# When a part's first expert block is let in, in a fused graph layer and mixture-of-experts kernel on one Trainium2 core

## The reference, cut to what matters

```
h   = layernorm(x)
agg = segment_sum(h[src] * edge_weight, dst)          # 12500 x 256
x   = x + agg @ W.T + b
z   = layernorm(x)
p   = softmax(z @ gate_w + gate_b); keep the two largest of 8 per node
for e in experts:  acc += cw[:, e] * (gelu(z @ W1[e] + b1[e]) @ W2[e] + b2[e])
x   = x + acc
```

## Time and profile before

| | us |
|---|---|
| median of the three runs | 2642.3 |
| the profiled execution, its time | 2648.2 |
| its span | 2646.6 |
| its mean granted clock of PE | 0.897 |
| PE busy / DVE busy / POOL busy | 2072.6 / 1590.4 / 1809.6 |
| ACT busy / PEld busy | 655.6 / 1629.8 |

### The profile page before, as it was taken

The page is one execution under the profiler, slowest core; times in us unless marked ns, Lnnn a source line. Parts: engine busy times, 40 slices in busy tenths (PEclk is TensorE's granted clock), DMA queues, the critical chain, the costliest instruction groups (busy, mean ns, idle before and its releaser), DMA issues.

```text
span 2646.6 us, 46928 instructions
## 1 busy us (share of the span) xinstructions
PE 2072.6 (78%) x11178; PEld 1629.8 (62%) x11179; DVE 1590.4 (60%) x6566; ACT 655.6 (25%) x1900; POOL 1809.6 (68%) x1909
## 2 busy tenths in 40 slices
PE   4665686698789788887985999886879878887585
PEld 2444464486577676665863778764667666665474
DVE  7888445365365365364563554675776756685475
ACT  2332121132122132221221223221222222223121
POOL 7665777777767767767766666767777777751473
PEclk8767898899899899998998999998989889998797
DMA  8766756877858768768768679677789797886697
GB/s 286 244 199 208 238 165 189 264 224 229 265 182 290 240 197 275 251 206 280 231 221 253 210 249 319 216 248 238 258 292 305 230 304 254 282 248 198 224 305 248
DMA packets 304350, 646.04 MB, mean 244 GB/s; under 512 B 62536, under 2 KB 197226, under 8 KB 291402
## 3 DMA queue, kind: packets, MB, share of 16 engines
q1 hardware_dynamic: 145320, 325.55, 36.4%
q0 software_dynamic: 90384, 248.17, 31.5%
q10 hardware_dynamic: 68370, 69.23, 7.5%
HBM read 543.70 MB, written 208.20 MB: 284 GB/s over the span
## 4 chain that ended last, share of the span: by engine, by line
PE 27%; DVE 20%; DMA 16%; SPq 15%; issue 11%; POOL 9%; ACT 1%; DVEq 1%; ACTq 0%; POOLq 0%
SPq L500 13%; DMA slots<-stage 10%; PE bank L881 9%; POOL rows L519 8%; PE bank L974 7%; PE bank L958 6%; DMA stage<-sorted_x 3%; DVE spread L1362 2%; DVE bn L1341 1%; PE bank L901 1%; POOL got L560 1%; DMA xi<-slots 1%; SPq L450 1%; PE bank L945 1%; DVE square_n L1409 1%
## 5 line engine op out<-in xcount | busy, mean ns | idle before, releaser
L519 POOL DMA_INDIRECT rows<-xhat,src_t x1488 | 1428.1, 960 | 561.3 <-issue 441.1
L881 PE MATMUL bank<-rows,spread 128*80 128x256 f32 x3328 | 869.7, 421 | 150.0 <-issue 77.9
L881 PEld LDWEIGHTS bank<-rows,spread 128*80 128x80 f32 x3328 | 549.4, 169 | 431.9 <-issue 210.6
L974 PE MATMUL bank<-w,hT 128*128 x1736 | 438.3, 398 | 56.9 <-DVE y_sb L1589 34.9
L958 PEld LDWEIGHTS bank<-xiT,w 128*128 128x128 f32 x3472 | 428.8, 195 | 30.8 <-DMA w<-in_w 7.0
L958 PE MATMUL bank<-xiT,w 128*128 128x128 f32 x3472 | 432.7, 279 | 11.6 <-DMA w<-in_w 5.8
L1375 DVE TENSOR_TENSOR acc<-acc,bank 128x160 f32 x208 | 67.0, 322 | 593.1 <-PE bank L871 520.0
L1162 ACT ACTIVATE hT<-bank,b1T 128x128 f32<-128x128 f32 x868 | 248.3, 368 | 701.4 <-PE bank L958 501.0
L974 PEld LDWEIGHTS bank<-w,hT 128*128 128x128 f32 x1736 | 326.4, 198 | 110.6 <-issue 71.3
L1362 DVE TENSOR_SCALAR spread<-iota_w,dst_rel,wgt 128x80 f32<-128x80 f32 x1488 | 366.3, 338 | 0.4
L519 POOL DMA_INDIRECT rows<-in_x,src_t x176 | 169.1, 961 | 77.6 <-issue 51.1
(11 more groups left out here) (191 smaller groups left out, 1854.6 us busy)
## 6 DMA issues: line engine op xcount, KB each, us to landing
w<-in_w SPq DMA_DIRECT2D x217, 512.0 KB
slots<-stage SPq DMA_DIRECT2D x760, 136.0 KB
xi<-slots SPq DMA_DIRECT2D x217, 136.0 KB, 4.4
stage<-sorted_x ACTq DMA_DIRECT2D x98, 272.0 KB
rows<-xhat,src_t POOLq DMA_INDIRECT x1488
yq<-y_sb ACTq DMA_DIRECT2D x182, 128.0 KB
x_t<-in_x SPq DMA_DIRECT2D x97, 128.0 KB
x_d<-x_t ACTq DMA_DIRECT2D x97, 128.0 KB
```

Of the source, the lines that this page charges most:

```text
L519: pool.indirect_dma_start(rows[q][:, c, :], None, x if g < RAW else xhat, bass.IndirectOffsetOnAxis(ap=src_t[:, g * CG + c:g * CG + c + 1] ...
L881: done = nc.tensor.matmul(B_SUM[0:W, 0:D], spread[g % 2][:, c, :], rows[q][:, c, :], start=c == 0, stop=c == CG - 1)
L974: done = nc.tensor.matmul(bank[:, 0:D], hT[i % 2][:, j, :], w2[:, bass.ds(e, 1), j, :].rearrange("p o f -> p (o f)"), start=j == 0, stop=j ...
```

## The change

One constant and one term in `plan`. A part's items no longer count as open in the turn after its last runs are sent, but one turn later than that, and three turns later for the last part of an epoch. This holds in busy turns alone. In turns with no gather the old rule stands.

```
@@ -67,6 +67,8 @@
 STAGES = 3
 
 SHARED = (range(0, 4), range(4, 8))
+
+ITEM_LAG = (1, 3)
 XI = 6
@@ -233,7 +235,7 @@
             if t.stage == PARTS[PART_OF[t.stage]][1] - 1:
                 sent_at[PART_OF[t.stage]] = tau
-        open_to = max([sure_items(k) for k in sent_at if sent_at[k] < tau], default=0)
+        open_to = max([sure_items(k) for k in sent_at if sent_at[k] + (ITEM_LAG[ends_epoch(k)] if busy else 0) < tau], default=0)
         waiting = open_to - item_next
```

## The result

The changed kernel takes 2581.93 us (median of 4 runs, 2574.24 to 2592.71) beside 2642.14 us of the kernel before on the same chip (the ratio leaves out its one run of 3464.66 us). The ratio is 0.9771 [0.9748, 0.9795]: 2.3% faster, 60 us, where 50 were forecast. The profiled execution took 2580.72 us with a span of 2579.1 us at a mean granted clock of 0.909 (before: 2648.2, 2646.6, 0.897).

The account below looks back on a forecast made before the run. POOL's gathers were taken to set the busy turns, with PE costing time only where POOL stood for it. Busy turns -70.5 us and the tail +20.4 gave -50, hence 2592 us against the median 2642.3; range 2566 to 2634.

Parts of the forecast that it names:

- the 3 us taken off for uneven turns: Busy turns: 3 us deducted from the gains because early in a part PE is not always right behind POOL.
- Part 8's loss: Part 8's start: part 7's items end later, one more double step meets the heavy turns, losing 3.8 us.
- the 26: Parts 6 and 7: PE starts right behind POOL, not 20 us behind, winning 26 of 38.3 us of stalls.
- the tail turn: Behind the gathers: one turn more of three items with index, batch and stores, costing 15.3 us.
- Three gather buffers cover them: Busy turns: PE's remaining waits, at most 1 to 3 us each at parts 1 to 5, were costed at nothing.
- 13 us of room: Parts 6 and 7: two turns of gathers, less landing of rows and sums, leave PE 13 us of room.
- The look-ups: Turn 208: three more tiles in DVE's list ahead of the last addition, 1.7 us each, costing 5.1 us.
- The lower bound of the prediction: Behind the gathers: two items and three tiles more, 3.1 MB at 299 GB/s, would cost 10.4 us.
- Rival 1: Busy turns: PE's waits come back nearly in full, some -75 us likely, giving 2567 us; chance 12%.
- Rival 2: Place turns: stalls belong to these, not to the waits, so only -5 us in all, 2637 us; chance 22%.
- Rival 3: Next part's place turn: postponed items meet it, three double steps add 3.8 us each, slower at 2649 us; chance 5%.
- Rival 4: Parts' starts: runs land later by what was won, PE meets the same wait a turn later, 2655 us; chance 3%.

Follow-up runs that it names:

- e4: Changed kernel with the lag only for parts of epoch 0, later parts by the old rule; 2576.33 us, ratio 0.9745.
- e8: Changed kernel with the lag only in epoch 0 and one look-up instead of four in turn 208; 2569.71 us, ratio 0.972.
- e6: Kernel before, without lag, with four gather buffers instead of three and four combining buffers instead of six; 2622.21 us, ratio 0.9908.
- e7: Changed kernel with four gather buffers instead of three and four combining buffers instead of six; 2567.53 us, ratio 0.9696.
- e11: As e8, but with no double step in turns that sort a tile; 2573.82 us, ratio 0.9753.
- e1: Changed kernel without the one-turn lag of ordinary parts, keeping three turns at an epoch's end; 2621.4 us, ratio 0.9937.
- e2: Changed kernel with a lag of one turn everywhere, at an epoch's end too; 2592.95 us, ratio 0.9822.
- e3: Changed kernel with longer lags, three turns for ordinary parts and five at an epoch's end; 2595.69 us, ratio 0.9832.
- e10: Kernel before, without lag, leaving out half of the second expert multiplication, so it computes something else; 2621.3 us, ratio 0.9916.
- e9: As e8, with four gather buffers instead of three and four combining buffers instead of six; 2548.77 us, ratio 0.9627.

## Why the prediction was right

**The bound, and the mechanism.** Right in the busy turns, and right in sign behind them. PE's waits for items fell to 11.7 us (under 25 expected). POOL's waits fell to 31.4 us (43 expected), the last gather came 81 us earlier (70 expected), and the part behind grew by 14 us (20 expected). A turn of PE later was enough for each wait of 11 us and less, three for the one of 23.4; the one at 2090 us stayed and cost POOL nothing. How near the 31.4 lie to the 43 is partly chance. e4 and e8 have the changed kernel's plan up to turn 164, and from turn 27 to there POOL waited 31.3 us in the changed kernel's trace, 32.5 in e8's and 43.2 in e4's.

**Part by part.** The gains of the sum, as stated and as the earlier trace rows and the rows after give them, with parts 6 to 8 by turns:

| part | stated | measured |
|---|---|---|
| 1 | 4.6 | 2.5 |
| 2 | 8 | 8.6 |
| 3 | 14 | 15.6 |
| 4 | 4 | 7.2 |
| 5 | 13 | 13.2 |
| 6 and 7 | 26 | 28.9 |
| 8 | -3.8 | -1.8 |
| taken off | -3 | 0 |
| sum | 62.8 | 74.2 |

The rule behind the numbers, the smaller of the stall and of how much earlier PE comes, holds. The miss of 11.4 us is spread over four terms that were too cautious: part 4 (3.2), where 3.8 were charged for a double step in a heavy turn, parts 6 and 7 (2.9), part 8 (2.0), and the 3 us taken off for uneven turns. Part 8's loss did come, at half its size. With e4's 15.6 us or e8's 10.2 us of stalls in parts 6 and 7, in place of 9.4, their gain would be 22.7 or 28.1, so differences of 3 us are within what two traces differ by. The right reason for the 26 is seen too: in turn 135 PE's sums end 8.5 us behind the start of that turn's gather, where it was 20.8. Of the two terms called the weakest this one was right and the tail turn was not (below).

**The fetches.** Three fewer at 2.5 us: with 74.2 of stalls they make 81.7, and 81.3 were measured.

**The buffers.** "Three gather buffers cover them" was the weak sentence. The number came out well only because almost no wait was left to cover, which is luck as far as the buffers go. e6 shows that a buffer covers no wait of PE as long as PE with its waits is slower than POOL over the whole part: the fourth one gave its lead once. The figure of 13 us of room in parts 6 and 7 gave the right gain all the same, since it is how far behind POOL PE starts, and not the size of the buffer, that the lag changed.

**The price behind the gathers.** 20.4 us stated, 13.9 measured. The look-ups were right: 5.1 stated, 5.0 as a longer wait, 5.3 by e8. The whole turn of 15.3 was mis-sized. A turn more cost 10.8 us from the first late item on, 12.2 between e6 and e7, which differ by the same edit, and 11.7 each in e11. The step that was wrong is "one turn more of three items": item 187 still enters in turn 211 in the changed kernel's plan, 188 is the first of turn 212, and behind the last runs the trace has 29 items, not 30. The turn more is one with two items. The five full turns took 77.2 us, as before, so full turns are not cheaper. The lower bound of the prediction, 10.4 us from the bytes of two items and three tiles, counted what is really added and came near; that the bytes are the reason was not tested. The whole price is less sure than its parts: between e6 and e7 the part behind the last gather grew by 19.5 us, near the 20.4 stated.

**The sum.** In the spans -67.5 us against -50: 10.8 from the busy turns (81.3 against 70.5) and 6.5 from the tail, both on the same side. The medians give -60, since the profiled execution of before lay 6 us above its median and the one of after 1.2 below. So the case came out at 2.3%, just beyond the 2% that the forecast's own cases were split by.

**The rivals.** Rival 1, the waits back nearly in full, was the nearest of the four: of 105.6 us 74 came back, in place turns too. Its 2567 is 15 us from the measured time, the forecast's 2592 is 10. Rival 2 is refuted: stalls at place turns fell with the lag and only in the parts that had one (e1 against e2), though DVE's work there is the same. Rival 3's mechanism is small with the lag of the change (1.8 us at part 8) and seen with the longer lag of e3. Rival 4 is refuted by the 1.19 us at part 3: the runs landed no later.

## What to carry to other kernels

Where two engines run one behind the other with buffers between them, compare the time that each takes for a whole period, waits included (here 186.6 against 170.9 us for 17 turns): if the follower is slower, a deeper buffer gives its lead once, and a wait taken out of the follower is won up to the difference. A postponed start cost next to nothing here as long as it was not longer than the wait it replaced; with three turns of lag it met the next heavy turns. Count the work that runs out of the steady turns item by item before charging a whole turn for it (here two items and 10.8 us, not three and 15.3), and short work that waits for nothing must not stand in front of the one operation that ends the steady part.

## What was not expected of the hardware

Over these runs PE's mean granted clock rises with how much it is kept busy: 0.878 at 75% of the span (e10), 0.897 at 78% (before), 0.909 at 80% (after) and 0.912 at 81% (e9). A long wait of PE is paid a second time behind it: the same four multiplications took 2.05 us behind 6.20 us of waiting and 1.10 us behind 1.22. The granted clock of the first was 0.50, the lower of the two levels (1.2 GHz), and that of the second 1.00 (between 2396.4 and 2398 us). The stretch of the first, in the changed kernel:

```profile
2320.00:2322.20 2.20, 2.08 (x6) 1.65 (x7) 0.81 (x4) 0.00 (x0) 0.00 (x0) 0.50 0.87 283
```

The mean clock fell where work was taken out (e10's sums took 409 ns each between 865 and 1415 us, before 401) and rose where waits were.

Two traces of kernels that hold the same instructions up to a turn can be 8 us apart by then, and over 13 in one case: the gather of turn 164 starts 7.8 us later in e4 than in the changed kernel, and 13.3 later than in e8. A difference of a few us in one trace is not yet an effect.
